# Scores of two heads side by side in 64-row tiles, from two float32r parts, through one ring of three bank pairs

## The reference

```python
# layer 0 (mask over keys) and layer 1 (strictly causal), 16 heads of 16, batch 8, 512 x 256
scores = einsum('bqhd,bkhd->bhqk', qp, kp) / 4          # layer 1: of its own projections
scores = where(mask == 0, -10000, scores)               # layer 1: keep j < i, and (0, 0)
attn   = softmax(scores, axis=-1)
ctx    = einsum('bhqk,bkhd->bqhd', attn, vp)            # then @ Wo + bo, added to x
# layer 0 goes on with a quantized ternary product, layer 1 with a gated FFN whose
# activations and weights are quantized (scales are maxima over whole tensors)
```

## Time and profile before

| | us |
|---|---|
| median of three executions | 1360.74 |
| profiled execution | 1357.38 |
| its span | 1355.6 |
| TensorE busy | 1256.7 (93%) |
| VectorE busy | 1001.9 (74%) |
| ScalarE busy | 867.9 (64%) |
| GpSimd busy | 512.4 (38%) |

### The profile page before, as it was taken

The page is one execution under the profiler, slowest core; times in us unless marked ns, Lnnn a source line. Parts: engine busy times, 40 slices in busy tenths (PEclk is TensorE's granted clock), DMA queues, the critical chain, the costliest instruction groups (busy, mean ns, idle before and its releaser), DMA issues. The chain is left out here.

```text
span 1355.6 us, 21435 instructions
## 1 busy us (share of the span) xinstructions
PE 1256.7 (93%) x7567; PEld 651.0 (48%) x7571; DVE 1001.9 (74%) x1724; ACT 867.9 (64%) x1483; POOL 512.4 (38%) x674
## 2 busy tenths in 40 slices
PE   9999799999999999999999999999998999980498
PEld 5566423334343433434555445545553785430298
DVE  5876588797878788786666688888773564996864
ACT  4455337676767777677665655565553666868693
POOL 4555300144343444435465433333333101656600
PEclk9999969999999999999999999999999999995699
DMA  8999684323334243433434553343101001326233
GB/s 288 379 344 323 237 178 114 101 65 101 97 105 131 64 130 80 114 95 102 122 84 110 150 173 94 103 120 101 60 18 48 1 0 47 140 93 232 78 109 109
DMA packets 88194, 170.82 MB, mean 126 GB/s; under 512 B 14866, under 2 KB 49430, under 8 KB 86550
## 3 DMA queue, kind: packets, MB, share of 16 engines
q1 hardware_dynamic: 87547, 168.16, 39.8%
q10 hardware_dynamic: 539, 1.26, 0.4%
HBM read 108.26 MB, written 60.31 MB: 124 GB/s over the span
## 5 line engine op out<-in xcount | busy, mean ns | idle before, releaser
L1341 DVE TENSOR_REDUCE b_neg_max<-b_score 128x1 f32<-128x512 f32 (+3 forms) x864 | 541.3, 663 | 177.6 <-PE b_score L886 93.5
L1111 ACT ACTIVATE b_probs<-b_exp 128x512 f32<-128x512 f32 (+1 forms) x864 | 463.2, 581 | 281.8 <-PE b_exp L910 281.1
L883 PE MATMUL b_score<-b_k_stack,b_q_stack 97*128 97x512 bf16 (+3 forms) x1024 | 356.0, 351 | 14.7 <-issue 8.8
L910 PE MATMUL b_exp<-b_q_stack,b_k_stack 100*128 100x512 bf16 (+3 forms) x1024 | 344.5, 341 | 6.4 <-ACT b_probs L1111 5.5
L931 PE MATMUL b_av<-b_probs,b_values 128*17 128x512 f32 (+3 forms) x2048 | 228.5, 518 | 3.7 <-POOL b_probs L1209 3.4
L883 PEld LDWEIGHTS b_score<-b_k_stack,b_q_stack 97*128 97x128 bf16 x1024 | 99.8, 98 | 250.5 <-DVE b_neg_max L1341 128.2
L910 PEld LDWEIGHTS b_exp<-b_q_stack,b_k_stack 100*128 100x128 bf16 x1024 | 100.1, 98 | 82.9 <-ACT b_probs L1111 24.9
L1209 POOL TENSOR_SCALAR_AFFINE_SELECT b_probs<-b_probs 128x512 f32<-128x512 f32 x96 | 61.7, 643 | 176.8 <-ACT b_probs L1111 176.2
L1217 POOL CAST b_max_parts<-b_neg_max 128x16 bf16<-128x16 f32 x64 | 12.9, 202 | 286.2 <-DVE b_neg_max L1341 283.9
L886 PE MATMUL b_score<-diag_qk,minus_big 128*128 128x128 bf16 x512 | 112.6, 220 | 0.0
L1625 PE MATMUL f_bank<-normed,f_w_upT 128*128 128x512 f32 x192 | 82.7, 592 | 0.0
(11 more groups left out here) (231 smaller groups left out, 2021.5 us busy)
## 6 DMA issues: line engine op xcount, KB each, us to landing
b_q_stack<-s_q SPq DMA_DIRECT2D x384, 64.0 KB
s_k<-a_part_k SPq DMA_DIRECT2D x48, 256.0 KB, 3.2
b_k_stack<-s_k SPq DMA_DIRECT2D x61, 192.0 KB
s_up<-f_up SPq DMA_DIRECT2D x6, 1536.0 KB, 5.1
s_va<-a_va SPq DMA_DIRECT2D x16, 544.0 KB, 5.5
b_values<-s_va SPq DMA_DIRECT2D x16, 544.0 KB, 4.4
a_mask_q<-mask_in SPq DMA_DIRECT2D x8, 1024.0 KB, 8.3
b_k_stack<-s_k SPq DMA_DIRECT2D x61, 128.0 KB
```

The lines of the kernel that those rows point to most:

```text
L883: mm = pe.matmul(o, q, KS[half][0:R_MAX, h, 0:w], start=True, stop=causal or not general)
L910: mm = pe.matmul(o, k, QS[half][0:NSTACK, h, q0:T], start=True, stop=not masked)
L1111: nc.scalar.activation(probs[kc][:, h0:h0 + m, q0:T], exp_bank[n % RINGS][:, 0:m * w].rearrange("p (h n) -> p h n", h=m), ACT.Exp).then_in ...
L1341: nc.vector.tensor_reduce(neg_max[u][:, qt, h0:h0 + m], score_bank[n % RINGS][:, 0:m * w].rearrange("p (h n) -> p h n", h=m), AX.X, ALU.ma ...
```

## The change

Queries and keys have two float32r parts. A head's stack is 51 rows (high x high, unseen keys, low, maximum) and fits in 64 partitions, so two heads lie side by side in the two halves of the array (`tile_rows`), in one instruction each, and `maxima` and `exponents` run at even steps only. Each pair fills two banks at once, one per head. One ring of three such bank pairs takes the place of the six banks: maxima, exponents, `turn_max` and `turn_out` all take the next pair, and a fill waits for the reader of the fill three places before, whichever engine that is (`wait_ring`). VectorE and ScalarE read both banks of a pair in one instruction. The causal mask of a diagonal block is added by four matmuls of 64 rows for two heads, the right half of the columns apart (`diagonal`). The maxima have two parts and two DMAs. Stacks are loaded by six DMAs for queries, four for keys and two for unseen keys. In the projection phase the third part and its copy go, and parts are stored as two float32 tensors instead of three bfloat16. The diff, cut to its core:

```diff
-PARTS = 3
-NSPLIT = 6 * HD
-R_KEY = NSPLIT
-R_MAX = NSPLIT + 1
+PARTS = 2
+R_KEY = 2 * HD
+R_LOW = R_KEY + 1
+R_MAX = R_LOW + HD
 NSTACK = R_MAX + PARTS
+HALF = P // 2
+PAIRS = H // 2
+QUERY_ROWS = ((0, 0), (HD, 0), (R_LOW, 1))
+KEY_ROWS = ((0, 2), (R_LOW, 1))
...
+def tile_rows(r, a, b):
+
+    return slice(HALF * r + a, HALF * r + b)
...
             def store_parts(b, n):
-                sp.wait_ge(remains[n], third(n, b, pieces(n) - 1))
                 for i in range(PARTS):
-                    sp.dma_start(dealt_rows(scratch[n[0]][batch_of(n, b)][i]), part[n][b % 2][:, i, :, :].rearrange("p c n -> p (c n)")).then_inc(parts_stored[n][b % 2], 16)
+                    if i == 0:
+                        sp.wait_ge(rounded[n], taken(b, DC - 1))
+                    else:
+                        sp.wait_ge(remains[n], rest_made(n, b, DC - 1))
+                    sp.dma_start(dealt_rows(scratch[n[0]][batch_of(n, b)][:, i]), part[n][b % 2][:, i, :, :].bitcast(F32)).then_inc(parts_stored[n][b % 2], 16)
...
-                next_part(b, "k0")
-                next_part(b, "k1")
...
-        score_bank = [pb(f"score{i}", [P, T], F32) for i in range(RINGS)]
-        exp_bank = [pb(f"exp{i}", [P, T], F32) for i in range(RINGS)]
+        ring = [pb(f"ring{i}", [P, 2, T], F32) for i in range(RINGS)]
...
-            shared = [{P: 4, 2 * P: 2}.get(x, 1) for x in widths[layer]]
-            MAX_FILLS.append([(qt, h, shared[qt]) for qt in range(TT) for h in range(0, 4, shared[qt])])
-            EXP_FILLS.append([(kc, h, shared[TT - 1 - kc]) for kc in range(TT) for h in range(0, 4, shared[TT - 1 - kc])])
+            shared = [min(2, T // x) for x in widths[layer]]
+            MAX_FILLS.append([(qt, i, shared[qt]) for qt in range(TT) for i in range(0, 2, shared[qt])])
+            EXP_FILLS.append([(kc, i, shared[TT - 1 - kc]) for kc in range(TT) for i in range(0, 2, shared[TT - 1 - kc])])
...
+        score_fill, exp_fill, fills, readers = {}, {}, {}, []
+
+        def add_fill(reader, name):
+
+            reader[name] = len(reader)
+            fills[name] = len(readers)
+            readers.append((score_read if reader is score_fill else exp_done, reader[name] + 1))
+
         for t in SLOTS:
             for s in range(STEPS):
-                if there(t + 2):
+                if there(t + 2) and s % 2 == 0:
                     f, place, m = fill_of(MAX_FILLS, t + 2, s)
                     if place == 0:
-                        score_fill["max", t + 2, f] = len(score_fill)
-                if s == TURN_OUT and there(t - 1):
-                    score_fill["out", t - 1] = len(score_fill)
-                if there(t):
+                        add_fill(score_fill, ("max", t + 2, f))
+                if there(t) and s % 2 == 0:
                     f, place, m = fill_of(EXP_FILLS, t, s)
                     if place == 0:
-                        exp_fill["exp", t, f] = len(exp_fill)
+                        add_fill(exp_fill, ("exp", t, f))
                 if s == turn_max_at(t) and there(t + 1):
-                    exp_fill["max", t + 1] = len(exp_fill)
+                    add_fill(exp_fill, ("max", t + 1))
+                if s == TURN_OUT and there(t - 1):
+                    add_fill(score_fill, ("out", t - 1))
+
+        def ring_of(name):
+            return ring[fills[name] % RINGS]
+
+        def wait_ring(pe, name):
+
+            if fills[name] >= RINGS:
+                pe.wait_ge(*readers[fills[name] - RINGS])
...
-            h0, h1 = 4 * g, 4 * g + 4
-            for row, i in ((0, 0), (1, 0), (2, 0), (3, 1), (4, 1), (5, 2)):
-                eng.dma_start(QS[n % 2][HD * row:HD * (row + 1), h0:h1, :], scratch["q"][n][i][:, h0:h1, :]).then_inc(stack_landed[n % 2][g], 16)
+            for r in range(2):
+                for row, i in QUERY_ROWS:
+                    eng.dma_start(QS[n % 2][tile_rows(r, row, row + HD), 2 * g:2 * g + 2, :].bitcast(F32), scratch["q"][n][r][i][:, 2 * g:2 * g + 2, :]).then_inc(stack_landed[n % 2][g], 16)
...
+                    if s % 2:
+                        return
...
-                    n = score_fill["max", t, f]
-                    if place == 0 and n >= RINGS:
-                        pe.wait_ge(score_read, n - RINGS + 1)
+                    if place == 0:
+                        wait_ring(pe, ("max", t, f))
                     w = widths[layer_of(t)][qt]
-                    o = score_bank[n % RINGS][:, place * w:(place + 1) * w]
-                    q = QS[half][0:R_MAX, h, qt * P:(qt + 1) * P]
-                    mm = pe.matmul(o, q, KS[half][0:R_MAX, h, 0:w], start=True, stop=causal or not general)
+                    o = ring_of(("max", t, f))[:, :, place * w:(place + 1) * w]
+                    for r in range(2):
+                        rows = tile_rows(r, 0, R_MAX)
+                        mm = pe.matmul(o[:, r, :], QS[half][rows, i, qt * P:(qt + 1) * P], KS[half][rows, i, 0:w], start=True, stop=causal or not general)
                     if causal:
-                        d = const["diag"][1 if qt == 0 else 0]
-                        mm = pe.matmul(o[:, w - P:w], const["minus_big"][:, :], d[:, :], start=False, stop=True, skip_group_check=True)
+                        mm = diagonal(t, s)
                     elif general:
-                        pe.matmul(o, const["minus_big"][:, :], DQ[half][:, qt, :], start=False, stop=False)
-                        mm = pe.matmul(o, const["less"][R_KEY:R_KEY + 1, 0:P], KS[half][R_KEY:R_KEY + 1, h, :], start=False, stop=True)
+                        for r in range(2):
+                            rows = tile_rows(r, R_KEY, R_KEY + 1)
+                            pe.matmul(o[:, r, :], const["minus_big"][:, :], DQ[half][:, qt, :], start=False, stop=False)
+                            mm = pe.matmul(o[:, r, :], const["less_r"][rows, 0:P], KS[half][rows, i, :], start=False, stop=True)
                     if place == m - 1:
...
+                def diagonal(t, s):
+
+                    qt = s // 4
+                    f, place, m = fill_of(MAX_FILLS, t, s)
+                    end = (place + 1) * widths[1][qt]
+                    for upper in range(2):
+                        for r in range(2):
+                            rows = tile_rows(r, 0, HALF)
+                            d = const["first_diag_half" if qt == 0 else "diag_half"][upper][r]
+                            mm = pe.matmul(ring_of(("max", t, f))[:, r, end - P + HALF * upper:end], const["big_half"][upper][r][rows, :], d[rows, HALF * upper:P],
+                                           start=False, stop=True, skip_group_check=True)
+                    return mm
...
-                    n = exp_fill["exp", t, f]
-                    if place == 0 and n >= RINGS:
-                        pe.wait_ge(exp_done, n - RINGS + 1)
+                    if place == 0:
+                        wait_ring(pe, ("exp", t, f))
                     q0 = P * kc if causal else 0
                     w = T - q0
-                    o = exp_bank[n % RINGS][:, place * w:(place + 1) * w]
-                    k = KS[half][0:NSTACK, h, kc * P:(kc + 1) * P]
+                    o = ring_of(("exp", t, f))[:, :, place * w:(place + 1) * w]
                     masked = general and not causal
-                    mm = pe.matmul(o, k, QS[half][0:NSTACK, h, q0:T], start=True, stop=not masked)
+                    for r in range(2):
+                        rows = tile_rows(r, 0, NSTACK)
+                        mm = pe.matmul(o[:, r, :], KS[half][rows, i, kc * P:(kc + 1) * P], QS[half][rows, i, q0:T], start=True, stop=not masked)
...
-                            nc.scalar.activation(probs[kc][:, h0:h0 + m, q0:T], exp_bank[n % RINGS][:, 0:m * w].rearrange("p (h n) -> p h n", h=m),
-                                                 ACT.Exp).then_inc(exp_done, 1)
+                            nc.scalar.activation(probs[kc][:, :, q0:T].rearrange("p (i r) n -> p r i n", r=2)[:, :, i0:i0 + m, :],
+                                                 ring_of(("exp", t, f))[:, :, 0:m * w].rearrange("p r (i n) -> p r i n", i=m), ACT.Exp).then_inc(exp_done, 1)
...
-                nc.gpsimd.tensor_copy(p[:, :, 0, :], m[:, :, :]).then_inc(max_chain, 1)
-                pool.wait_ge(max_chain, 3 * t + 1)
-                nc.gpsimd.tensor_tensor(max_rest[:, :, :], m[:, :, :], p[:, :, 0, :], ALU.subtract).then_inc(max_chain, 1)
-                pool.wait_ge(max_chain, 3 * t + 2)
-                nc.gpsimd.tensor_copy(p[:, :, 1, :], max_rest[:, :, :]).then_inc(max_chain, 1)
-                pool.wait_ge(max_chain, 3 * t + 3)
-                nc.gpsimd.tensor_tensor(p[:, :, 2, :], max_rest[:, :, :], p[:, :, 1, :], ALU.subtract).then_inc(max_split, 1)
+                nc.gpsimd.tensor_copy(p[:, :, :, 0, :], m[:, :, :, :]).then_inc(max_chain, 1)
+                pool.wait_ge(max_chain, t + 1)
```

(33 more changed lines are left out.)

238 lines of the change are left out of this document (111 added, 127 removed).

## The result

The changed kernel takes 1496.03 us (median of 4 runs, 1480.14 to 1499.14) against 1359.7 before: a ratio of 1.097 [1.089, 1.105]. It is slower, as forecast, but by seven times the forecast 19 us, and outside the range of 1328 to 1408.

A forecast was written before the change was run, and what follows sets the result against it. TensorE was taken to bound slots with projections, others being near both TensorE and VectorE. Terms -10 + 28 - 1 - 2 + 4 = +19 on 1357.38 gave 1376.4, stated as 1378 us for the median; range 1328 to 1408.

The forecast's parts named there:

- the fixed order in one ring: Attention: all fills share three bank pairs, each waiting for the reader three places before; plain layer-0 slot 12.8 against 12.54 us.
- VectorE idle in spite of less to read: Sign of being right: VectorE's waits before the reads rise from 178 us although there are fewer reads.
- waits ahead of Ed: Layer 1: the fourth exponent fill waits for a maxima read, delaying group and next maxima; VectorE idle 1.9 us there.
- -10: Layer 0 in sum: 7 batches at -1.65 us and 5 plain slots at +0.3 us.
- Once risen it stayed at 2.4 GHz where TensorE was busy 6.8 of 8.0 us.: Clock after the hand-over: earlier trace rows read as showing that, once up, it stays up.
- the +4 for the clock: Start of attention: the clock rises one slot later, +4 us, bounds 0 and +25.
- the clock rival: Waits keep TensorE at 1.2 GHz from the first score pair: 1400 us for five slots, nearly 1700 for all; chance 0.08.
- Layer 1, +28.: Layer-1 slots in sum: 5 batches at +3.15 us and 3 quantizing ones at +4.2 us.
- The drains I leave at 0 net.: Drains between tile shapes, set against overlapping reads: 0 net, up to +25 us or down to -10.
- The -3.4 for shorter loads and maxima slots: Hand-over and start: -1 us for SP's fewer stores and one more load, -2.4 for two slots holding maxima alone.
- Projections: Projection phase: dropping third parts and copies gains nothing beside a busy TensorE; larger stores 0, bounds -1 and +10.
- DMA: Rival: projection phase becomes bound by transfers once a batch needs over 18.6 us of queues; 1388 us, chance 0.05.

The follow-up runs named there:

- crossed: Changed kernel without the ring of bank pairs and merged reads: six single banks, one head's score beside the other's exponent matmul; 1375.6 us, 1.015.
- hold2: Changed kernel plus five zero matmuls per layer-1 slot, in TensorE's idle time before the exponent pair that waits for a VectorE read; 1434.9 us, 1.055.
- warm_start: Changed kernel plus 32 zero matmuls in the two slots that hold maxima alone; 1490.3 us, 1.096.
- c_full: The kernel without the ring, with layer-1 masks moved straight behind each score matmul and made full-height (128 rows); 1835.4 us, 1.352.

## Why the prediction was wrong

- *Direction and cause* were right: the fixed order in one ring, VectorE idle in spite of less to read, waits ahead of Ed. crossed shows it. The size was not: 137 us on the profiled executions instead of 19. Of the 118 us missing, layer 1 has 91.5 (119.5 against 28), layer 0 has 20.5 (+10.5 against -10) and the start 6.2 (7.2 against 1).
- *"Once risen it stayed at 2.4 GHz where TensorE was busy 6.8 of 8.0 us."* This step failed, and with it the +4 for the clock: in layer 1 the clock did not stay. I derived waits of 2 us in each layer-1 slot for VectorE and never asked what TensorE's share of them does to the clock, and I gave the clock rival its price only for a rise that never came. Profiled, hold2's layer 1 is 51 us shorter (from slot 30: 810.1 against 861.1 us), and its clock still dips now and then, so the clock cost at least about that. An estimate from the slots: where a slot of the same number or kind ran at 1.00 in this trace, in warm_start's or in hold2's, I put its length in place. Slots 30 to 60 then take some 429 us, against 484 measured and 381 before, so some 55 us are clock and some 48 the rest. The trace agrees with the Trainium skill, "TensorE: Matmul & The Clock Gate", section "A second HAM failure mode: psum-queue depth-cycling", here: the granted clock swings between 1.00 and 0.50 behind waits of 1.1 us or more for a bank. I had cited that rule and not followed it. c_full's fall without visible idle time goes beyond it.
- *Layer 1, +28.* At the full clock a quantizing batch takes 54.0 us, not 51.7: +6.5 and not +4.2 on 47.5; over layer 1 the estimate above gives some 48. Much of it lies in the product slot: slot 42, which doesn't quantize, takes 16.03 us at the full clock, and I had 14.5 for its kind.
- *"The drains I leave at 0 net."* Mis-sized. At the full clock the group starts 0.43 us after the exponent pair (I used 0.31), and the read behind it starts 0.61 after the score pair (I used 0.5). So a round with a group takes 2.02 us instead of 1.80, and a plain layer-0 slot has three that wait: 0.7 us of the 1.04 by which it missed. The rest isn't traced, and no run separates a drain from a weight load of 0.19 us behind a wait. Plain slots took 13.84 us (12.8 forecast) and product slots 16.17 (15.0). A batch was 60.3 us, not 58.05: layer 0 gave +10 without the start, not -10.
- *Start.* Slot 1 took 18.33 us, where such a slot takes 13.84 at the full clock: the late rise cost 4.5 us, near the +4 forecast. That is partly luck, as hold2's slot 1 took 14.39 without any change there. The -3.4 for shorter loads and maxima slots did not come: slot 0 began 1.4 us later. TensorE stood idle for 5.0 us up to 174 us, while the next stacks were loaded; that these were the cause was not tested.
- *Slips.* 1376.4 and 3.4 make 1379.8, not 1378, and the fourteen score matmuls of the earlier trace rows come one per 0.56 us, not 0.61. Neither changes the argument.
- *Projections* cost nothing, as said. The *DMA* rival did not occur. Of the rivals *the clock* was nearest, by another road than mine: it gave 1400 to 1700 for a clock that stays down from the start. It deserved far more than 0.08.

What stays open: how the 48 us in layer 1 that are not clock divide between waits and changes of mode; whether the order in the ring or the merged reads weigh more; and what exactly the clock looks at. That pairs of 64-row tiles as such keep it down is excluded: crossed holds 1.00 through all of layer 0 after slot 1, and so does the changed kernel.

## What to carry to other kernels

Count a PSUM ring in read times: a bank is held for its hand-over (0.6 us here) and its read, so six single banks with own rings hid most of what three pairs in one ring exposed (1375.6 against 1496.0 us). Before merging reads, check which in-order wait then stands ahead of a long matmul group. Where a change adds a single idle stretch of some 1.3 us to TensorE's slot, price the slot at both clocks; several of 0.9 us did no harm to the clock here. Two heads in 64-row tiles can share a step without sharing a bank pair, by crossing score and exponent; a 128-row matmul between them undoes it.

## What the runs showed of the hardware

A busy share of 100% in the profile does not mean that the clock stays up: it fell in c_full at 648.4 us with no idle time shown, and came back for long only in slots with output products (means of 0.69 to 0.76 there, 0.50 to 0.55 in the others from slot 33 to 61). Five matmuls of 0.22 us in one 1.3 us stall a slot gave back 61 us of 1496, with a mean clock of 0.952 instead of 0.891. A 128-row mask between 64-row float32r matmuls took a head's step from 0.35 to 0.87 us at the full clock.
